# Two of the shared expert's first eight tiles moved from beside the second way back to beside the second path sums

## Chip, cores and metric

The kernel runs on one core of one Trainium2 chip. The metric is the device time of one execution in microseconds (us); several executions are timed and their median is taken. Engines are called as in the profile: PE is TensorE (matmul), PEld its weight loads, DVE is VectorE, ACT is ScalarE, POOL is GpSimd, SP is SyncE, which here issues most DMAs.

## What is computed

Input `x` is (32, 64, 256), the context `ctx` (32, 1601, 256). Three residual blocks follow one another, each on the layer norm of `x`:

```
x = x + xattn(ctx, layernorm(x))     # per sample: euclidean distances, time-warping table, way back,
                                     # context rows of the path summed into the 64 rows they meet
x = x + attn(layernorm(x))           # gated linear recurrence over time, 16 heads, output projection
x = x + ffn(layernorm(x))            # 8 routed experts, top 2 of them, and a shared expert that all rows use
...
def _ffn(x, w1, w2, w3):
    h = jax.nn.silu(x @ w1.T) * (x @ w3.T)
    return h @ w2.T
...
D = _pairwise_euclidean(small, large)
R = _dtw_cost(D)
i_idx, j_idx, valid = _backtrack(R, T_small, T_large)
```

The hidden width of an expert is 704. The 2048 rows of `x` make 16 tiles of 128; the shared expert works on all 16.

## The kernel before

**Alignment.** The 32 samples go in two groups of 16. For a group DVE fills a table step by step (71 steps), and then walks the way back, 71 more steps in which each needs the one before it (L718 shuffle, L719, L724, in the first steps walked also L729). After it a few small operations and one of 1024 columns (L799) write `path_terms`, and a count (`spread`) lets TensorE begin with the group's path sums.

**Path sums** (`add_rows`, TensorE L1469, L1487). They go by pairs of samples, 16 pairs, of which pairs 8 to 15 belong to the second group. A pair has two halves, seven and six 128-row pieces of the context: 14 and 12 matmuls of 256 columns in the program, recorded as 28 and 24 in the trace. Each half needs three things: a mask `on_path`, which TensorE prepares two halves ahead (`path_weigh`, L1465, into banks 2 and 3) and ACT finishes with three activations (`path_mask`, L1200, L1201, L1204); two loads of context rows (`rows_c`), which SP issues into a ring of five (`load_rows`, L1829 and L1832), each when the half that used its slot before has been read (`rows_read`); and a bank that is free. The sums of a pair stand in bank 0 or 1 by turns, and DVE adds them to `xr` (L808).

**Recurrence** (`recurrence(c)`, c from 0 to 3) works on four tiles at once; it uses banks 4 and 5.

**Shared expert** (`experts`, with `up` L1629, `turn` L1640, `down` L1655 on TensorE). A tile is done in two halves of 352 hidden columns. For half h, `up` makes two products into banks 2·(h mod 2) and 2·(h mod 2)+1; ACT takes Silu of the one (L1287, `act_s`), DVE multiplies with the other (L905, `hid`); `turn` transposes the result into bank 6, ACT and DVE copy it out (L1294 and L912, `hidT`); `down` sums into bank 7, and after the second half DVE adds bank 7 to `xr` (L920, `take_output`). The steps run as a pipeline: one step of `experts` is `up` of half h, `turn` of h-1, `down` of h-2, and two more steps drain it.

**Order of the work.** It is written out by hand, the same on each engine. All engines run their programs in order; generators `interleave`, `beside`, `together` and `chain` say after how many steps of one part a step of another comes. The part around the change, which stands alike in the programs of DVE (L1111), ACT (L1377) and TensorE (L1798):

```
interleave(align(1), chain(add_rows(range(0, 4)), together(recurrence(0), add_rows(range(4, 8))),
                           beside(recurrence(1), experts(RUNS[0]), shared_beside), experts(RUNS[1])),
           behind_second)
run(add_rows(range(8, 12)))
run(together(recurrence(2), add_rows(range(12, 16))))
last_recurrence()
```

`RUNS[0]` is tiles 0 to 3 of the shared expert, `RUNS[1]` tiles 4 to 7, `RUNS[2]` tiles 8 to 11, which `last_recurrence` does itself; the routed tiles and tiles 12 to 15 come last. Late in the way back `behind_second` gives one step of `experts` for every four steps of the way back. SP's program has none of the expert's steps and only follows `rows_read` with its loads.

Of the kernel before, what the change touches and what calls it, by code (L numbers as in the profile page):

```python
# [122 lines left out]
def run(steps):  # L123
    for _ in steps:
        pass
# [85 lines left out]


def half_chunks(n):

    return range(n % 2 * CTH, min(CT, (n % 2 + 1) * CTH))
# [11 lines left out]
def rec_order(others):  # L227
# [3 lines left out]

RUNS = [[("shared", t) for t in range(0, 4)], [("shared", t) for t in range(4, 8)],
        [("shared", t) for t in range(8, 12)], [("routed", t) for t in range(MOE_TILES)], [("shared", t) for t in range(12, 16)]]
# [6 lines left out]
def build(nc, x, ctx_nat, ctx_tr, wr_t, wk, wv_t, ww_t, wo_t, gate_t, w1_t, w3_t, w2_t, out):  # L240
    stack = ExitStack()
    with stack:
# [225 lines left out]
        def code_rows(g, q, h):  # L468
            steps = half_steps(q, h)
            return code[g][:, steps[0]:steps[-1] + 1, 0:L]  # L470

        def shared_x(t, k):
# [89 lines left out]
        def vector_program(e):  # L562
# [238 lines left out]
            def add_rows(pairs):  # L801
                for pair in pairs:
                    for _ in range(4):
                        yield
                    e.wait_ge(rows_read, 2 * (pair + 1))
                    if pair == 0:
                        e.wait_ge(x_in, 16)
                    e.tensor_tensor(xr[:, pair, :], xr[:, pair, :], psum[pair % 2][:, 0:D], ALU.add).then_inc(added, 1)  # L808
                    yield
# [89 lines left out]
            def gate_hidden(h):  # L899
                i = h % 2  # L900
                e.wait_ge(upped, 2 * h + 2)
                e.wait_ge(silued, h + 1)
                if h >= 2:
                    e.wait_ge(hid_crossed, h - 1)
                e.tensor_tensor(hid[i][:, :], psum[2 * i + 1][:, 0:HH], act_s[i][:, :], ALU.mult).then_inc(hid_done, 1)  # L905

# [190 lines left out]
            def add_shares():  # L1097
                for n, t in enumerate(SHARES):
                    e.wait_ge(back_in[t // CTILES], 16)
                    e.wait_ge(y_done, UNIT_OF["shared", t if t in (12, 13) else 11] + 1)  # L1100
                    for k in range(2):
# [15 lines left out]
            run(experts(RUNS[3]))  # L1117
            interleave(experts(RUNS[4]), add_shares(), lambda n: 0 if n < 2 else 2 if n < 6 else 3)


        def scalar_program(e):
# [160 lines left out]
            def silu_hidden(h):  # L1282
                i = h % 2
                e.wait_ge(upped, 2 * h + 1)
                if h >= 2:
                    e.wait_ge(hid_done, h - 1)
                e.activation(act_s[i][:, :], psum[2 * i][:, 0:HH], ACT.Silu).then_inc(silued, 1)  # L1287

# [24 lines left out]
            def last_recurrence():  # L1313
# [53 lines left out]
                for unit in range(2, 4):  # L1367
                    for h in range(2):
                        silu_hidden(first[unit] + h)
                    for h in range(2):  # L1370
# [8 lines left out]
                       behind_second)  # L1379
            run(add_rows(range(8, 12)))  # L1380
            run(together(recurrence(2), add_rows(range(12, 16))))
            last_recurrence()
            run(experts(RUNS[3]))
            run(experts(RUNS[4]))


        def tensor_program(e):
# [62 lines left out]
            def path_weigh(n):  # L1450
# [18 lines left out]
            def add_rows(pairs):  # L1469
                for pair in pairs:  # L1470
# [3 lines left out]
                    if pair >= 2:  # L1474
                        e.wait_ge(added, pair - 1)
                    if pair == 8:

                        e.wait_ge(hid_done, 2 * 8)
                    for half in range(2):
# [4 lines left out]
                        for t in half_chunks(half):  # L1484
                            k = min(P, N - t * P)
                            for b in range(2):
                                last = e.matmul(psum[pair % 2][b * T:(b + 1) * T, 0:D],  # L1487
                                                on_path[(2 * pair + half) % 3][0:k, t - half * CTH, b * T:(b + 1) * T],
                                                rows_c[loads[b] % ROWS_RING][0:k, t - half * CTH, :],
                                                start=(t == 0), stop=(t == CT - 1))  # L1490
# [21 lines left out]
            def recurrence(c):  # L1512
# [89 lines left out]
            def up(h, kind, t, half, ex):  # L1602
# [16 lines left out]
                for m in range(2):  # L1619
                    if h >= 2 and m == 0:  # L1620
                        e.wait_ge(silued, h - 1)
                    elif h >= 2:
                        e.wait_ge(hid_done, h - 1)
                    for k in range(KC):
                        if kind == "shared":
                            lhsT, rhs = shared_x(t, k), ws_up[:, m, k, half * HH:(half + 1) * HH]
                        else:
                            lhsT, rhs = srcT[t % 2][:, k, :], w_up[:, bass.ds(ex, 1), m, k, half * HH:(half + 1) * HH]
                        last = e.matmul(psum[2 * i + m][:, 0:HH], lhsT, rhs, start=(k == 0), stop=(k == KC - 1))  # L1629
                    last.then_inc(upped, 1)  # L1630
# [161 lines left out]
            for u in range(GUNITS):  # L1792
                distance_products(u)
                if u in LATENTS_AT:
# [5 lines left out]
                       behind_second)  # L1800
            run(add_rows(range(8, 12)))
            run(together(recurrence(2), add_rows(range(12, 16))))
            last_recurrence()
            run(experts(RUNS[3]))
            run(experts(RUNS[4]))


# [189 lines left out]
```

## Time and profile before

| | |
|---|---|
| median of 3 runs | 1258.32 us (1256.58 to 1264.05) |
| the profiled execution | 1258.05 us, of which the span from first to last instruction is 1256.6 us |
| mean granted TensorE clock | 0.921 of full speed |
| busy: PE, DVE, ACT | 1018.7 us (81%), 703.5 us (56%), 485.3 us (39%) |
| DMA, mean over the span | 143 GB/s |

Stages of the span that matter here, in microseconds from its start: up to 711 the second group's table and way back with other work beside it; 711 to 809 the second group's path sums (together with the recurrence of tiles 8 to 11 from 754 on); 809 to 897 the last recurrence and the routing; from 897 the routed experts and the last shared tiles, in which TensorE is busy without a break.

A timeline row gives start, duration, engine, line, operation, output<-inputs, the shapes and the number of instructions merged in it; in square brackets stands how long the engine was idle before, and what ended that.

### The profile page before, as it was taken

To read this page: it belongs to the slowest core of one execution; us is meant where nothing else is said; L and a number is where in the kernel's file an instruction comes from. 1 tells how busy PE (TensorE), PEld (TensorE's weight loads), DVE (VectorE), ACT (ScalarE), POOL (GpSimd) and SP (SyncE) were. 2 spreads that over 40 slices of the span, in tenths; PEclk is the share of its full clock that TensorE was granted. 3 is DMA by queue.
4 is the path that set the end of the run, shared out by engine and by line. 5 is a ranking of instruction groups with operands and counts; after the bars stand their busy time and mean duration, and the time that the engine had idled before them with its cause. 6 is when DMAs were issued, how large, how long until landed. Compare 5 with 4: busy or idle time off the path is not lost. (4 is left out here: it accounts for less than half of the span.)

```text
span 1256.6 us, 15701 instructions
## 1 busy us (share of the span) xinstructions
PE 1018.7 (81%) x4832; PEld 618.0 (49%) x4832; DVE 703.5 (56%) x2431; ACT 485.3 (39%) x854; POOL 83.6 (7%) x113
## 2 busy tenths in 40 slices
PE   5876636988662599987889578887899999999998
PEld 2332212333220255543656355545677777777776
DVE  5756729999899677496569602346322222222226
ACT  4855434676763244423322144242122222222221
POOL 1000000000000000000000000000122222222210
PEclk9978968999986799989889699889899999999999
DMA  9999974777986979530000098394010011110105
GB/s 365 262 238 289 212 148 134 178 182 177 192 219 99 311 241 329 177 122 1 0 17 1 8 344 277 126 366 170 22 34 31 32 31 34 34 34 30 30 31 192
DMA packets 117407, 179.76 MB, mean 143 GB/s; under 512 B 7600, under 2 KB 91024, under 8 KB 117072
## 3 DMA queue, kind: packets, MB, share of 16 engines
q1 hardware_dynamic: 113584, 168.54, 46.8%
q0 software_dynamic: 3744, 10.23, 2.5%
q8 instruction: 42, 0.69, 0.2%
q14 instruction: 37, 0.30, 0.1%
HBM read 154.32 MB, written 24.42 MB: 142 GB/s over the span
## 5 line engine op out<-in xcount | busy, mean ns | idle before, releaser
L1629 PE MATMUL bank<-w_up,srcT 128*128 x624 | 197.4, 459 | 0.6 <-ACT srcT L1279 0.6
L905 DVE TENSOR_TENSOR hid<-bank,act_s 128x352 f32<-128x352 f32 x110 | 57.4, 524 | 213.6 <-PE bank L1629 208.5
L1416 PE MATMUL bank<-sq,ones 128*64 128x402 f32 (+1 forms) x512 | 107.5, 543 | 48.8 <-ACT sq L1146 48.8
L1629 PEld LDWEIGHTS bank<-w_up,srcT 128*128 128x128 f32 x624 | 117.8, 189 | 54.9 <-issue 0.8
L1287 ACT ACTIVATE act_s<-bank 128x352 f32<-128x352 f32 x110 | 50.8, 464 | 224.5 <-PE bank L1629 224.5
L1432 PE MATMUL bank<-table,ident 128*128 128x402 f32 x144 | 67.1, 550 | 74.1 <-DVE stays L673 67.2
L1410 PE MATMUL bank<-ctxT,latT 128*64 128x402 f32 (+1 forms) x512 | 108.3, 547 | 19.2 <-DMA ctxT<-ctx_tr_dram 18.4
L1655 PE MATMUL bank<-w_dn,hidT 128*128 (+1 forms) x468 | 114.0, 380 | 0.4 <-DVE y_sb L926 0.4
L1487 PE MATMUL bank<-rows_c,on_path 128*64 128x256 f32 (+1 forms) x832 | 100.5, 394 | 11.5 <-DMA rows_c<-ctx_nat_dram 10.7
L1146 ACT ACTIVATE sq<-ctxT 128x1608 f32<-128x1608 f32 x64 | 97.5, 1526 | 11.9 <-DMA ctxT<-ctx_tr_dram 11.9
L1179 ACT ACTIVATE code<-bank,unpassed 128x402 bf16<-128x402 f32 x72 | 42.4, 593 | 135.6 <-PE bank L1434 135.6
L1416 PEld LDWEIGHTS bank<-sq,ones 128*64 128x64 f32 x512 | 36.1, 147 | 116.9 <-ACT sq L1146 78.6
L703 DVE TENSOR_TENSOR_SCAN table<-col_min,table 128x201 f32<-128x201 f32 x140 | 88.6, 633 | 2.6
L1655 PEld LDWEIGHTS bank<-w_dn,hidT 128*128 128x128 f32 (+1 forms) x468 | 83.1, 191 | 8.7 <-issue 0.6
L1629 PE MATMUL bank<-ws_up,h2T 128*128 128x352 f32 x256 | 85.8, 485 | 0.0
L1487 PEld LDWEIGHTS bank<-rows_c,on_path 128*64 128x64 f32 (+1 forms) x832 | 62.5, 141 | 46.4 <-issue 22.3
L1294 ACT ACTIVATE hidT<-bank 128x256 f32<-128x256 f32 x110 | 42.3, 384 | 86.4 <-PE bank L1640 86.4
L1410 PEld LDWEIGHTS bank<-ctxT,latT 128*64 128x64 f32 x512 | 37.0, 147 | 77.0 <-issue 55.1
L1432 PEld LDWEIGHTS bank<-table,ident 128*128 128x128 f32 x144 | 25.6, 203 | 100.0 <-issue 92.3
L696 DVE TENSOR_TENSOR col_min<-table 128x201 f32<-128x201 f32 x142 | 50.9, 359 | 40.0 <-DMA table<-spaced 21.9
L1629 PEld LDWEIGHTS bank<-ws_up,h2T 128*128 128x128 f32 x256 | 51.0, 202 | 25.4 <-issue 4.2
L1433 PE MATMUL bank<-col_min,less 128*128 128x402 f32 x144 | 63.3, 523 | 0.0
(255 smaller groups left out, 1448.5 us busy)
## 6 DMA issues: line engine op xcount, KB each, us to landing
rows_c<-ctx_nat_dram SPq DMA_DIRECT2D x32, 896.0 KB
ctxT<-ctx_tr_dram SPq DMA_DIRECT2D x32, 804.0 KB, 10.0
ctxT<-ctx_tr_dram SPq DMA_DIRECT2D x32, 797.0 KB, 10.7
rows_c<-ctx_nat_dram SPq DMA_DIRECT2D x32, 640.0 KB
table<-spaced SPq DMA_DIRECT2D x16, 896.4 KB, 12.2
spaced<-dist SPq DMA_DIRECT2D x128, 101.0 KB, 6.7
w_up<-w_t_dram SPq DMA_DIRECT2D x16, 704.0 KB, 12.2
w_dn<-w_t_dram SPq DMA_DIRECT2D x16, 256.0 KB, 4.8
```

The source lines that it names most:

```text
L696: e.tensor_tensor(low, prev[:, 1:W], prev[:, 0:L], ALU.min).then_inc(step_done, 1)
L703: e.tensor_tensor_scan(cur[:, 1:W], low, cur[:, 1:W], first, ALU.min, ALU.add).then_inc(step_done, 1)
L905: e.tensor_tensor(hid[i][:, :], psum[2 * i + 1][:, 0:HH], act_s[i][:, :], ALU.mult).then_inc(hid_done, 1)
L1146: e.activation(sq[i][:, :, :, 0:nq], ctxT[ctx_slot(n)][:, :, :, q * QC:q * QC + nq], ACT.Square).then_inc(squared, 1)
L1287: e.activation(act_s[i][:, :], psum[2 * i][:, 0:HH], ACT.Silu).then_inc(silued, 1)
L1410: last = e.matmul(ps[b * T:(b + 1) * T, 0:nq], latT[:, k, pair * P + b * T:pair * P + (b + 1) * T], ctxT[ctx_slot(n)][:, b, k, half * QC:h ...
L1416: last = e.matmul(ps[b * T:(b + 1) * T, 0:nq], ones[:, 0:T], sq[i][:, b, k, 0:nq], start=False, stop=(k == KC - 1))
L1432: e.matmul(gap, ident[:, :], table[g][:, k0 + 1:k0 + n + 1, 0:L], start=True, stop=False)
L1433: e.matmul(gap, less[:, :], col_min[i][:, 2 * h:2 * h + n, :], start=False, stop=False)
L1487: last = e.matmul(psum[pair % 2][b * T:(b + 1) * T, 0:D], on_path[(2 * pair + half) % 3][0:k, t - half * CTH, b * T:(b + 1) * T], rows_c[l ...
L1629: last = e.matmul(psum[2 * i + m][:, 0:HH], lhsT, rhs, start=(k == 0), stop=(k == KC - 1))
L1655: last = e.matmul(psum[7][:, 0:D], hidT[i][0:r, c, :], rhs, start=(half == 0 and c == 0), stop=(half == 1 and c == HC3 - 1))
```

## The change

Tiles 6 and 7 of the shared expert leave the run that is interleaved with the way back and become a run of their own, `RUNS[2]`, beside the path sums of pairs 8 to 11. (The later runs get the numbers 3 to 5, and all units keep their order.) The new rule `path_beside` gives one step of `experts` after the path sums' steps 1, 4, 7, ... (counted from 0; a pair has five). Since banks 0 to 3 are in use by the path sums there, these four halves put their eight products into banks 1, 4 and 5 by turns, and the sums of pairs 8 to 11 all stand in bank 0. With that a pair's sums must wait until the pair before has been added (pairs 9 to 12), pair 8 waits for six tiles rather than eight, pair 12 and the recurrence of tiles 8 to 11 wait until the expert's halves 12 to 15 have been read. SP's and POOL's programs are unchanged.

```
+def path_beside(n):
+
+    return 1 if n % 3 == 1 else 0
...
-RUNS = [[("shared", t) for t in range(0, 4)], [("shared", t) for t in range(4, 8)],
+RUNS = [[("shared", t) for t in range(0, 4)], [("shared", t) for t in range(4, 6)], [("shared", t) for t in range(6, 8)],
...
+        beside_sums = 2 * UNIT_OF["shared", 6]
+
+        def up_bank(h, m):
+
+            if beside_sums <= h < beside_sums + 4:
+                return psum[(1, 4, 5)[(2 * (h - beside_sums) + m) % 3]]
+            return psum[2 * (h % 2) + m]
+
+        def sum_bank(pair):
+            return psum[0 if 8 <= pair < 12 else pair % 2]
...
-            run(add_rows(range(8, 12)))
+            run(beside(add_rows(range(8, 12)), experts(RUNS[2]), path_beside))
...
                 if n == 2 * GTILES:

-                    e.wait_ge(hid_done, 2 * 8)
-                    e.wait_ge(hidT_act, 2 * 8)
-                    e.wait_ge(hidT_dve, 2 * 8)
-                    e.wait_ge(y_done, 8)
+                    e.wait_ge(hid_done, 2 * 6)
...
                     if pair >= 2:
-                        e.wait_ge(added, pair - 1)
-                    if pair == 8:
-
-                        e.wait_ge(hid_done, 2 * 8)
+                        e.wait_ge(added, pair if 9 <= pair <= 12 else pair - 1)
+                    if pair == 8 or pair == 12:
+
+                        e.wait_ge(hid_done, 2 * 6 if pair == 8 else 2 * 8)
...
+                    if c == 2 and h == 0:
+
+                        e.wait_ge(silued, 2 * 8)
+                        e.wait_ge(hid_done, 2 * 8)
...
-                    if h >= 2 and m == 0:
+                    job = 2 * (h - beside_sums) + m
+                    if 0 <= job < 3:
+                        if m == 0:
+
+                            e.wait_ge(hid_done, beside_sums)
+                            e.wait_ge(h2_turned, 4)
+                            e.wait_ge(gate_own, GATE_OWN + 1)
+                    elif 3 <= job < 8:
+                        e.wait_ge(silued, h) if m else e.wait_ge(hid_done, h - 1)
+                    elif h >= 2 and m == 0:
                         e.wait_ge(silued, h - 1)
```

How the instructions move is shown at two places. The first is DVE within the second way back, where a step of `experts` stood between two steps of it (L718 to L724 are one step; `hid`, `hidT` and the sum into `xr` are the expert's). Before:

```order
L718 STREAM_SHUFFLE beyond<-threshold_68 128x1
L719 SCALAR_TENSOR_TENSOR beyond<-row_53,threshold_68 128x201
L724 ISA passed,threshold_68<-beyond,code_107 128x202
L724 ISA threshold_68 128x1
L905 TENSOR_TENSOR hid_152<-bank,act_s_150 128x352
L912 COPY hidT_153<-bank 96x128
L920 TENSOR_TENSOR xr<-xr,bank 128x256
L718 STREAM_SHUFFLE beyond<-threshold_68 128x1
```

The same place after the change (its lines are 16 higher):

```order
L734 STREAM_SHUFFLE beyond<-threshold_68 128x1
L735 SCALAR_TENSOR_TENSOR beyond<-row_53,threshold_68 128x201
L740 ISA passed,threshold_68<-beyond,code_107 128x202
L740 ISA threshold_68 128x1
L936 TENSOR_TENSOR xr<-xr,bank 128x256
L734 STREAM_SHUFFLE beyond<-threshold_68 128x1
```

Here tile 5 is being drained: its last sum stays, while the multiplication and the copy of tile 6 are gone. Over the whole way back four `hid`, four `hidT` and two `xr` go.

The second place is TensorE between the sums of pair 9 and those of pair 10 (the number after `bank` is the bank's own). Before:

```order
L1487 MATMUL bank1<-rows_c3_142,on_path1_145 64x256
L1487 MATMUL bank1<-rows_c4_143,on_path1_145 64x256
L1465 MATMUL bank2<-path_terms_147,row_terms_148 128x128 x4
L1465 MATMUL bank3<-path_terms_147,row_terms_148 128x128 x2
L1487 MATMUL bank0<-rows_c0_139,on_path2_146 64x256
L1487 MATMUL bank0<-rows_c1_140,on_path2_146 64x256
```

After:

```order
L1478 MATMUL bank3<-path_terms_147,row_terms_148 128x128 x2
L1655 MATMUL bank4<-ws_up_169,h2T1_172 128x352 x2
L1655 MATMUL bank5<-ws_up_169,h2T1_172 128x352 x2
L1666 MATMUL bank6<-ident_49,hid1_152 128x128 x2
L1666 MATMUL bank6<-ident_49,hid1_152 96x128
L1681 MATMUL bank7<-ws_dn_170,hidT0_153 128x256 x3
L1655 MATMUL bank1<-ws_up_169,h2T1_172 128x352 x2
L1655 MATMUL bank4<-ws_up_169,h2T1_172 128x352 x2
L1666 MATMUL bank6<-ident_49,hid0_151 128x128 x2
L1666 MATMUL bank6<-ident_49,hid0_151 96x128
L1681 MATMUL bank7<-ws_dn_170,hidT1_154 128x256 x3
L1500 MATMUL bank0<-rows_c0_139,on_path2_146 64x256
```

Two whole steps of `experts` (the third and the fourth of the six) now stand in this one place. The others stand singly: an `up` after the first half of pair 8, `up` and `turn` after its second half, `turn` and `down` after pair 10, a last `down` after the first half of pair 11.

## Rows read from the trace of the kernel before

**Rows 1.** The page: its first line.

```profile
span 1256.6 us, 15701 instructions
```

**Rows 2.** Windows: stretch, us, busy of PE, PEld, DVE, ACT, POOL, clock, DMA share, GB/s.

```profile
656.00:695.00 39.00, 34.76 (x131) 23.52 (x132) 36.61 (x200) 6.43 (x16) 0.00 (x0) 0.94 0.00 1
711.00:720.00 9.00, 7.05 (x42) 4.45 (x42) 0.39 (x1) 3.73 (x6) 0.00 (x0) 0.55 0.01 2
730.00:740.00 10.00, 6.99 (x52) 4.83 (x48) 0.42 (x1) 2.67 (x4) 0.00 (x0) 0.83 1.00 348
750.00:760.00 10.00, 7.60 (x75) 5.46 (x72) 2.68 (x10) 5.01 (x8) 0.00 (x0) 1.00 1.07 370
772.00:790.00 18.00, 17.65 (x69) 7.88 (x69) 3.83 (x8) 8.79 (x14) 0.00 (x0) 1.00 0.50 168
```

**Rows 3.** Timeline of DVE in the second way back, eight of its steps.

```profile
671.52 0.52 DVE L905 TENSOR_TENSOR hid<-bank,act_s 128x352 f32<-128x352 f32 x1
671.96 0.28 DVE L912 COPY hidT<-bank 96x128 f32<-96x128 f32 x1
672.17 0.15 DVE L718 STREAM_SHUFFLE beyond<-threshold 128x1 f32<-128x1 f32 x1
...
673.11 0.15 DVE L718 STREAM_SHUFFLE beyond<-threshold 128x1 f32<-128x1 f32 x1
...
675.80 0.52 DVE L905 TENSOR_TENSOR hid<-bank,act_s 128x352 f32<-128x352 f32 x1
...
680.41 0.52 DVE L905 TENSOR_TENSOR hid<-bank,act_s 128x352 f32<-128x352 f32 x1
```

**Rows 4.** Timeline of PE, one step of `experts` where nothing stands between.

```profile
908.32 2.53 PE L1629 MATMUL bank<-w_up,srcT 128*128 x8
910.69 0.49 PE L1640 MATMUL bank<-ident,hid 128*128 128x128 f32 x3
911.02 1.46 PE L1655 MATMUL bank<-w_dn,hidT 128*128 x6
912.32 2.53 PE L1629 MATMUL bank<-w_up,srcT 128*128 x8
```

**Rows 5.** Timeline of PE over the path sums of pairs 8 to 13.

```profile
711.45 0.93 PE L1465 MATMUL bank<-path_terms,row_terms 128*128 128x128 f16 x7 [9.96 <-DVE path_terms L799]
...
714.67 5.39 PE L1487 MATMUL bank<-rows_c,on_path 128*64 128x256 f32 x28 [0.34 <-issue]
719.99 0.56 PE L1465 MATMUL bank<-path_terms,row_terms 128*128 128x128 f16 x7
720.49 2.81 PE L1487 MATMUL bank<-rows_c,on_path 128*64 128x256 f32 x24
723.24 0.51 PE L1465 MATMUL bank<-path_terms,row_terms 128*128 128x128 f16 x6
725.03 3.24 PE L1487 MATMUL bank<-rows_c,on_path 128*64 128x256 f32 x28 [1.29 <-DMA rows_c<-ctx_nat_dram]
728.21 0.56 PE L1465 MATMUL bank<-path_terms,row_terms 128*128 128x128 f16 x7
729.05 2.81 PE L1487 MATMUL bank<-rows_c,on_path 128*64 128x256 f32 x24 [0.28 <-DMA rows_c<-ctx_nat_dram]
...
735.31 4.93 PE L1487 MATMUL bank<-rows_c,on_path 128*64 128x256 f32 x28 [3.01 <-DMA rows_c<-ctx_nat_dram]
...
763.74 3.24 PE L1487 MATMUL bank<-rows_c,on_path 128*64 128x256 f32 x28 [1.62 <-DMA rows_c<-ctx_nat_dram]
```

**Rows 6.** The tile of context rows, 700 to 816: what its matmuls waited for.

```profile
  DMA rows_c<-ctx_nat_dram: 10.7, 9
```

**Rows 7.** DMA issues 711 to 809 (KB each), and a piece of the chain (start, us).

```profile
rows_c<-ctx_nat_dram SPq DMA_DIRECT2D x13, 896.0 KB
rows_c<-ctx_nat_dram SPq DMA_DIRECT2D x14, 640.0 KB
...
rows_c<-ctx_nat_dram SPq DMA_DIRECT2D x14, 65.0 KB
...
720.09 4.80 DMA rows_c<-ctx_nat_dram
```

**Rows 8.** Timeline of ACT and DVE: a copy, one mask's three activations, one sum.

```profile
694.98 0.38 ACT L1294 ACTIVATE hidT<-bank 128x256 f32<-128x256 f32 x1 [3.89 <-PE bank L1640]
...
743.96 0.60 ACT L1200 ACTIVATE on_path<-bank 128x512 f32<-128x512 f32 x1 [1.13 <-PE bank L1465]
744.45 0.38 ACT L1201 ACTIVATE on_path<-bank 128x256 f32<-128x256 f32 x1
744.87 0.93 ACT L1204 ACTIVATE on_path<-on_path,ones 128x768 f32<-128x768 f32 x1
752.32 0.42 DVE L808 TENSOR_TENSOR xr<-xr,bank 128x256 f32<-128x256 f32 x1 [8.37 <-PE bank L1487]
```

More of the change, by code:

```diff
@@ L807, in add_rows @@
                         e.wait_ge(x_in, 16)
-                    e.tensor_tensor(xr[:, pair, :], xr[:, pair, :], psum[pair % 2][:, 0:D], ALU.add).then_inc(added, 1)
+                    e.tensor_tensor(xr[:, pair, :], xr[:, pair, :], sum_bank(pair)[:, 0:D], ALU.add).then_inc(added, 1)
                     yield
@@ L904, in gate_hidden @@
                     e.wait_ge(hid_crossed, h - 1)
-                e.tensor_tensor(hid[i][:, :], psum[2 * i + 1][:, 0:HH], act_s[i][:, :], ALU.mult).then_inc(hid_done, 1)
+                e.tensor_tensor(hid[i][:, :], up_bank(h, 1)[:, 0:HH], act_s[i][:, :], ALU.mult).then_inc(hid_done, 1)
             def turn_hidden(h):
@@ L1113, in vector_program @@
                        behind_second)
-            run(add_rows(range(8, 12)))
+            run(beside(add_rows(range(8, 12)), experts(RUNS[2]), path_beside))
             run(together(recurrence(2), add_rows(range(12, 16))))
             last_recurrence()
-            run(experts(RUNS[3]))
-            interleave(experts(RUNS[4]), add_shares(), lambda n: 0 if n < 2 else 2 if n < 6 else 3)
+            run(experts(RUNS[4]))
+            interleave(experts(RUNS[5]), add_shares(), lambda n: 0 if n < 2 else 2 if n < 6 else 3)
         def scalar_program(e):
@@ L1286, in silu_hidden @@
                     e.wait_ge(hid_done, h - 1)
-                e.activation(act_s[i][:, :], psum[2 * i][:, 0:HH], ACT.Silu).then_inc(silued, 1)
+                e.activation(act_s[i][:, :], up_bank(h, 0)[:, 0:HH], ACT.Silu).then_inc(silued, 1)
             def turn_hidden(h):
@@ L1379, in scalar_program @@
                        behind_second)
-            run(add_rows(range(8, 12)))
+            run(beside(add_rows(range(8, 12)), experts(RUNS[2]), path_beside))
             run(together(recurrence(2), add_rows(range(12, 16))))
             last_recurrence()
-            run(experts(RUNS[3]))
             run(experts(RUNS[4]))
+            run(experts(RUNS[5]))
         def tensor_program(e):
@@ L1486, in add_rows @@
                             for b in range(2):
-                                last = e.matmul(psum[pair % 2][b * T:(b + 1) * T, 0:D],
+                                last = e.matmul(sum_bank(pair)[b * T:(b + 1) * T, 0:D],
                                                 on_path[(2 * pair + half) % 3][0:k, t - half * CTH, b * T:(b + 1) * T],
@@ L1628, in up @@
                             lhsT, rhs = srcT[t % 2][:, k, :], w_up[:, bass.ds(ex, 1), m, k, half * HH:(half + 1) * HH]
-                        last = e.matmul(psum[2 * i + m][:, 0:HH], lhsT, rhs, start=(k == 0), stop=(k == KC - 1))
+                        last = e.matmul(up_bank(h, m)[:, 0:HH], lhsT, rhs, start=(k == 0), stop=(k == KC - 1))
                     last.then_inc(upped, 1)
@@ L1800, in tensor_program @@
                        behind_second)
-            run(add_rows(range(8, 12)))
+            run(beside(add_rows(range(8, 12)), experts(RUNS[2]), path_beside))
             run(together(recurrence(2), add_rows(range(12, 16))))
             last_recurrence()
-            run(experts(RUNS[3]))
             run(experts(RUNS[4]))
+            run(experts(RUNS[5]))
         def sync_program(e):
```

## The prediction, as written before the run

> **What bounds the kernel now.** I read the page first, for the span of 1256.6 us [rows 1]; then the chain of waits, to see in which stage which engine ends last; then the windows, stage by stage; then the timelines of DVE, TensorE and ACT in the two stages that the change touches. The order of the two programs says what moved, never how long it takes.
>
> Two stages matter. In the second way back DVE sets the pace. In the 39.0 us from 656 to 695 DVE is busy for 36.61, and TensorE, at 34.76, works in the gaps that DVE's order gives it [rows 2]. No wait of DVE's stands between the steps: a step without an insert takes 673.11 - 672.17 = 0.94 us, and the timeline shows the next one starting at once [rows 3]. TensorE ends its share early and is idle for 9.96 us before the path sums can begin at 711.45 [rows 5]. So what DVE sheds here comes off the time, and what TensorE sheds does not.
>
> In the path sums that follow, the loads of context rows set the pace. TensorE waits for them nine times, 10.7 us in total [rows 6], and they move 370 GB/s at a full DMA share [rows 2]. From about 768 on the recurrence of tiles 8 to 11 joins in, and TensorE is the bound: 17.65 us busy of 18.0 [rows 2]. After that nothing of the change is left; whatever TensorE is late with at 768 it stays late with to the end.
>
> **Term 1: what the way back sheds.** A tile puts two steps of the expert between eight steps of the way back. From 671.52 to 680.41 is one such tile, 8.89 us; eight bare steps are 8 x 0.94 = 7.52; so a tile costs the way back 1.37 us, less than the durations of its five instructions together, because part of them fills the small gap between two dependent steps [rows 3]. Two tiles leave: 2 x 1.37 = 2.74 us. I bound it by 1.8 (if two of the inserts had filled gaps that stay) and 3.4 (four `hid`, four `hidT`, two sums into `xr` at their start-to-start distances of 0.44, 0.21 and 0.33). ACT's and TensorE's shares there were under cover and bring nothing. The path sums should start at 711.93 rather than 714.67.
>
> **Term 2: what TensorE has to do more afterwards.** One step of the expert at full clock goes from 908.32 to 912.32: 2.37 for the `up`, 0.33 for the `turn`, 1.30 for the `down`, 4.00 us in all [rows 4]. Four halves are 16.0 us. They enter a stretch where TensorE had been waiting. What it can swallow is in the rows.
>
> **Term 3: how much of it the waits take.** I walk TensorE's order. A pair at full clock, taken from start to start, is 3.18 for the first half, 0.50 for the next weighing, 2.75 for the second half, 0.45 for its weighing: 6.88 us [rows 5].
>
> From pair 8 to the start of pair 10, before: 735.31 - 714.67 = 20.64 us, in which 1.29 + 0.28 + 3.01 = 4.58 us are waits for loads [rows 5]. After: the same without these waits is 16.06; the first four steps of the expert (4 `up`, 3 `turn`, 2 `down`) add 9.48 + 0.99 + 2.60 = 13.07. That is 29.1 us. The five loads that are in the ring at the start and the four that follow have 29 us for what took under 21, so no load is late. Pair 10 starts at 711.93 + 29.1 = 741.1, that is 5.75 later than before.
>
> From pair 10 to the start of pair 13, before: 763.74 - 735.31 = 28.43 us [rows 5]. After, two roads lead there. TensorE's: three pairs, 20.64; the last two steps of the expert, 2.93; and two waits. The first is new: the `hidT` of half 15 stands on ACT behind a mask of 1.84 us (744.87 + 0.93 - 743.96), then 0.38 for it [rows 8], then DVE's copy and the sum of pair 10, 0.28 and 0.42 [rows 3, 8], and pair 11 now waits for that sum, because all four pairs use bank 0. With the hand-overs that is 2.9 us from the end of the weighing, of which 1.63 is covered by TensorE's own `turn` and `down`: 1.3 us seen. The second, at pair 12, is the sum of pair 11 alone, 0.42 and its hand-over less a weighing of 0.45: 0.4 seen. The road is 25.3 us. The loads' road: at pair 10 the ring is full, so nine loads must still pass before pair 13, five of 896 KB and four of 640 + 65 KB [rows 7], 7.47 MB; at 370 GB/s that is 20.2 us, after the first half of pair 10 (3.2) and a latency of 2.3 (the 4.80 us from issue to landing less the 2.48 that 896 KB take at that rate [rows 7]). 25.7 us. Neither road is met alone: a late load delays the next issue, which is why pairs before took some 9.5 us where the bytes ask for 8.8. I take the middle between the longer road and the 28.43 of before, 27.0, less a trace for the clock dip below: 26.9.
>
> Pair 13 then starts at 741.1 + 26.9 = 768.0 against 763.74 [rows 5]: 4.2 us later. The ends are 25.7 and 28.43, that is 3.0 and 5.75 later. (In other words: of 16.0 us some 9 vanish in waits and 2.7 come back from the way back.)
>
> **The clock.** The granted clock was 0.83 in 730 to 740, after the wait of 3.01 us, and the first half of pair 10 took 4.93 us instead of 3.24; in 711 to 720 it was 0.55 and the first half of pair 8 took 5.39 [rows 2, 5]. So each time TensorE fell to 1.2 GHz for a while. The 1.7 us at pair 10 are in the 28.43 above and should go, since TensorE no longer stands before pair 10; that is part of why I end below that figure. The 2.15 us at pair 8 I keep, though TensorE will now have been idle for some 28 us rather than 10 before it (the drained steps end near 680). The Trainium skill, page "TensorE: Matmul & The Clock Gate", section "HAM oscillation — how this bites in real kernels", says that waits for loads let the clock fall and that keeping the array busy across them holds it up; at pair 10 the trace agrees with its 0.83, and by that rule the dip goes as I have it, while without it the sum would be 1.7 us more.
>
> **The other edits.** The three banks by turns: each of the eight products needs a bank whose reader finished a whole step earlier; the nearest are the two adjoining steps, which follow each other as in the routed stage, where a step takes 4.00 us without a wait [rows 4]. I take 0, and bound it by 0 and 1. The waits at pair 12 and at the recurrence find everything read long ago: 0. ACT gets four Silu and four copies, some 3.4 us, into a stretch where it is busy for 5.01 of 10 [rows 2]: hidden, but for the mask above. No load is issued earlier or later for another reason than `rows_read`.
>
> **The sum.** -2.74 + 16.0 - 9.1 = +4.2 us on the profiled execution's 1258.05, that is 1262.25; the median of the runs is 0.27 above that execution, so 1262.5.
>
> **Rivals.**
> A. *The waits swallow all they can.* All 10.7 us of waits for loads, the 1.7 of the dip and the 2.15 of the cold start vanish: 16.0 - 14.55 - 2.74 = -1.3 us, 1257. For it speaks that the ring is full when the expert's steps end; against it that the loads after pair 10 have the same 7.47 MB to move and that the steps stand in the first half of the stretch.
> B. *The cold start lasts longer.* TensorE idles nearly three times as long before pair 8. If it stays at 1.2 GHz through the first two `up` and the second half of pair 8, then 2.37 + 2.75 + 2.37 us run at half speed and cost up to 7.5 more: 1270. For it: 0.55 in 711 to 720 [rows 2]. Against: 9.96 us of idle already led to the lower level, and it cannot go below that. Half of that price, 1266, is the likelier form.
> C. *The turns do not turn (slower by over 1%).* At each of five places TensorE waits for ACT's mask, then Silu or copy, then DVE: about 3 us that I take as covered everywhere but once. If the cover of an `up` were missing in all of them, 5 x 3 = 15 us come on top: 1277. It would decide from 1.7 us of idle time per step (8.4 us in all) on. Against it: the masks are made two halves ahead, and ACT has half its time free [rows 2].
>
> **Chances.** Forecast 0.62, A 0.16, B 0.13, C 0.06, something else 0.03. A measurement of this kernel tells about 1%, 12.6 us, from no change. The forecast, A and nearly all of B lie within it; C and the end of B give slower 0.06; nothing here reaches 12 us faster, which leaves 0.02 for what I don't see. The range takes in A with a microsecond of scatter, and B's likelier form with three: 1256 to 1269.
>
> **What would show it.** The path sums of pair 8 should start near 711.9, and pair 10 near 741, with no wait for a load before it and a clock of 1.00 there. Waits of the `rows_c` matmuls for DMA should fall from 10.7 us to about 3, all after pair 10. TensorE should wait for DVE's sum before pair 11, by 1 to 1.5 us. From pair 13 to the end everything should lie 4 us later and else be unchanged. I am wrong if the start of pair 8 has moved by less than 1.8 or more than 3.4, if waits for ACT or DVE add up to more than 4 us between pairs 8 and 12, or if the stage after pair 13 changes its own length.

## The result

| | median | runs |
|---|---|---|
| before | 1260.93 us (1250.46 to 1271.03) | 18 |
| changed | 1268.24 us (1258.36 to 1276.47) | 18 |

The ratio is 1.0059, with a 95% interval of 1.0030 to 1.0088: 7.4 us slower (3.8 to 11.1), within the 1% that the prediction calls no change. The two profiled executions differ by more: the span of the changed kernel's is 14.6 us over the 1256.6 of [rows 1]. How much of that is the change and how much the single execution is the question of what follows.

The page of the changed kernel begins, against [rows 1]:

```profile
span 1271.2 us, 15702 instructions
```

The windows of the changed kernel, against [rows 2] (stretch, us, busy of PE, PEld, DVE, ACT, POOL, clock, DMA share, GB/s):

```profile
695.00:711.00 16.00, 0.22 (x3) 0.23 (x4) 14.47 (x78) 0.00 (x0) 0.00 (x0) 0.50 0.00 0
711.00:720.00 9.00, 7.50 (x50) 4.89 (x49) 0.00 (x0) 4.17 (x7) 0.00 (x0) 0.63 0.00 0
730.00:740.00 10.00, 10.00 (x69) 6.75 (x66) 1.14 (x3) 4.57 (x8) 0.00 (x0) 1.00 0.91 303
740.00:750.00 10.00, 10.00 (x82) 6.62 (x82) 1.23 (x3) 3.19 (x6) 0.00 (x0) 1.00 0.42 142
```

TensorE now does nothing in the last 16 us of the way back (its 0.22 us lie behind 710.78), and works without a break from 730 to 750, at full clock, where before it was busy for 6.99 of the first 10 us at 0.83 and for 8.19 of the second 10 at 1.00. The loads moved 348 and 299 GB/s in these two windows before, and 303 and 142 now: they wait for TensorE to read what they brought.

TensorE's timeline over the pairs' first halves and the places where steps of the expert came in, against [rows 5]:

```profile
710.78 0.93 PE L1478 MATMUL bank<-path_terms,row_terms 128*128 128x128 f16 x7 [25.01 <-DVE path_terms L815]
...
714.00 5.03 PE L1500 MATMUL bank<-rows_c,on_path 128*64 128x256 f32 x28 [0.34 <-issue]
...
719.37 2.59 PE L1655 MATMUL bank<-ws_up,h2T 128*128 128x352 f32 x8
...
727.82 3.24 PE L1500 MATMUL bank<-rows_c,on_path 128*64 128x256 f32 x28
...
734.58 2.59 PE L1655 MATMUL bank<-ws_up,h2T 128*128 128x352 f32 x8
737.00 0.49 PE L1666 MATMUL bank<-ident,hid 128*128 128x128 f32 x3
737.33 1.46 PE L1681 MATMUL bank<-ws_dn,hidT 128*128 128x256 f32 x6
738.63 2.53 PE L1655 MATMUL bank<-ws_up,h2T 128*128 128x352 f32 x8
...
742.72 3.24 PE L1500 MATMUL bank<-rows_c,on_path 128*64 128x256 f32 x28
...
752.49 3.24 PE L1500 MATMUL bank<-rows_c,on_path 128*64 128x256 f32 x28 [1.21 <-DVE xr L824]
...
765.88 2.81 PE L1500 MATMUL bank<-rows_c,on_path 128*64 128x256 f32 x24 [1.15 <-DMA rows_c<-ctx_nat_dram]
...
770.38 3.24 PE L1500 MATMUL bank<-rows_c,on_path 128*64 128x256 f32 x28 [1.25 <-DMA rows_c<-ctx_nat_dram]
```

Pair 8 starts at 714.00, pair 10 at 742.72, pair 13 at 770.38. Two steps of the expert take 742.72 - 734.58 = 8.1 us including a short hand-over, against the 4.00 us each of [rows 4], so the turns of banks 1, 4 and 5 cost nothing. Pair 11 waits for DVE for 1.21 us. What the row names as DVE is a chain of three engines, here from the end of ACT's mask to TensorE:

```profile
750.58 0.94 ACT L1220 ACTIVATE on_path<-on_path,ones 128x768 f32<-128x768 f32 x1
751.42 0.36 ACT L1310 ACTIVATE hidT<-bank 128x256 f32<-128x256 f32 x1
751.82 0.29 DVE L928 COPY hidT<-bank 96x128 f32<-96x128 f32 x1 [8.58 <-ACT hidT L1310]
752.03 0.41 DVE L824 TENSOR_TENSOR xr<-xr,bank 128x256 f32<-128x256 f32 x1
```

The matmuls' waits for loads, 10.7 us in [rows 6], have shrunk to this (the tile of context rows, what it waited for):

```profile
  DVE xr L824: 3.2, 3
  DMA rows_c<-ctx_nat_dram: 2.6, 3
```

The first of these rows counts matmuls and weight loads together. Of the matmuls alone only one waited for DVE, pair 11's, 1.2 us.

**Where the 14.6 us are.** I cut every profile at the same events, so that stages can be compared whatever came before them: A, up to the `down` of the shared expert before which TensorE waits 4.41 us for DVE (655.77 before, the row below); B, from there to the end of `path_terms`; C, from the start of pair 8 (always 3.28 us later) to the crossing of the recurrence's rows (`ident,hn`) right behind the first half of pair 13; D, from there to the first routed `up`; E, the rest. The 3.28 us between B and C are in no column but in the span.

```profile
655.77 2.90 PE L1655 MATMUL bank<-ws_dn,hidT 128*128 128x256 f32 x6 [4.41 <-DVE hidT L912]
```

| profile | A | B | C | D | E | span |
|---|---|---|---|---|---|---|
| before | 655.8 | 55.6 | 52.6 | 131.4 | 357.9 | 1256.6 |
| changed | 657.8 | 52.9 | 60.0 | 139.4 | 357.9 | 1271.2 |
| difference | +2.0 | -2.7 | +7.3 | +8.0 | 0.0 | +14.6 |

A holds no change at all, so its difference is scatter. B and C hold the change. D has the same instructions in the same order, and was a surprise.

### The profile page after: what moved, and what is told of

It is laid out like the page before. It is cut to its first block, busy times and chain, and to the rows that moved or that the text cites. A ratio compares the mean times of both kernels' runs of the same rounds, so it can differ in the third digit from the quotient of the medians.

```text
span 1271.2 us, 15702 instructions
## 1 busy us (share of the span) xinstructions
PE 1027.0 (81%) x4832; PEld 624.0 (49%) x4832; DVE 705.2 (55%) x2431; ACT 484.3 (38%) x854; POOL 83.6 (7%) x113
## 4 chain that ended last, share of the span: by engine, by line
PE 40%; DVE 7%; ACT 1%; issue 1%; DMA 1%; DVEq 0%; ACTq 0%
PE bank L1655 18%; PE bank L1681 10%; PE bank L1500 3%; PE bank L1666 3%; PE bank L1521 2%; DVE beyond L735 2%; DVE passed L740 1%; DMA rows_c<-ctx_nat_dram 1%; PE bank L1615 1%; DVE beyond L734 1%; PE bank L1771 1%; PE bank L1478 1%; PE bank L1583 0%; PE bank L1601 0%; DVE hid L921 0%
## 5 line engine op out<-in xcount | busy, mean ns | idle before, releaser
L1500 PEld LDWEIGHTS bank<-rows_c,on_path 128*64 128x64 f32 (+1 forms) x832 | 59.2, 139 | 41.7 <-issue 13.6
```

Source lines behind the costliest of these rows:

```text
L1500: last = e.matmul(sum_bank(pair)[b * T:(b + 1) * T, 0:D], on_path[(2 * pair + half) % 3][0:k, t - half * CTH, b * T:(b + 1) * T], rows_c[l ...
```

## The experiments

Two profiles of one kernel are needed before a difference between two kernels means anything, so the first two runs repeat both.

**The kernel before, again.** No edit.

> The kernel before once more, unchanged. In the two profiles at hand the stretch from the end of pair 15 to the first routed tile took 90.1 us before and 96.7 us in the changed kernel, with the same instructions in the same order and a granted clock of 0.91 and 0.80 (817 to 913 us). Theory (that part is chance: where the clock falls differs from execution to execution): here the same stretch differs from 90.1 by 2 us or more, or the clock in it does. Rival (the change causes it): 90.1 within 0.5 us again.

A 653.0, B 55.6, C 51.8, D 134.2, span 1255.7 us. The stretch that the expectation speaks of took 91.6 us, 1.5 more than in the first profile, which is less than the 2 us that the theory asked for and more than the 0.5 that the rival allowed; D, which also takes in pairs 13 to 15, is 2.7 us longer. So D does scatter. B agrees to 0.1 us, and C to 0.9. The slow first half that pair 10 had in [rows 5] (4.93 us) is found at pair 11 here (4.62), so the place of this dip is not fixed either.

**The changed kernel, again.** No edit.

> The changed kernel once more, unchanged. Theory (chance): the stretch from the end of pair 15 to the first routed tile lies away from 96.7 us by 2 us or more, anywhere between 90 and 97; the stretch from pair 8 to pair 13 is again 56.4 within 0.5 us, since there TensorE does not stand still long enough for its clock to fall. Rival (the change causes the longer end stretch): 96.7 within 1 us again.

A 655.1, B 52.9, C 60.7, D 137.3, span 1267.2 us. B is -2.7 again, C is +9.0 against the second profile of before, and D is 2.1 us away from the first. From pair 8 to pair 13 it took 57.2 us, outside the 56.4 within 0.5 that was expected. The end stretch took 94.6 us, 2.1 less than the first time, just over the 2 us that the theory of chance had asked for. Yet D is longer in both profiles of the changed kernel than in both of before, which makes chance alone a weak explanation; the later runs take that up. Nearly all of the difference lies behind pair 15: that stretch took 90.1 and 91.6 us before, 96.7 and 94.6 in the changed kernel.

**Half of the change.** Only tile 7 moves.

```
-[("shared", t) for t in range(4, 6)], [("shared", t) for t in range(6, 8)],
+[("shared", t) for t in range(4, 7)], [("shared", t) for t in range(7, 8)],
...
-        beside_sums = 2 * UNIT_OF["shared", 6]
+        beside_sums = 2 * UNIT_OF["shared", 7]
...
-                    e.wait_ge(hid_done, 2 * 6)
+                    e.wait_ge(hid_done, 2 * 7)
```

> The change by half: only tile 7 of the shared expert moves beside the path sums, tile 6 stays beside the way back. Theory (what counts is how much TensorE work the waits for loads can swallow, some 9 us of it): the way back gains 1.37 us instead of 2.7; of 8.0 us of TensorE work added nearly all is swallowed, the stretch from pair 8 to pair 13 takes 50 to 51 us (before 49.1, changed 56.4), and the sum against the kernel before is -0.7 to +0.5 us. Rival (the steps cost by their number, through hand-overs and the bank turns, not by TensorE's time): half the loss of the changed kernel, so 52.7 us for the stretch and about +2.3 us in all.

B 54.2, C 54.6, D 131.1; ratio 1.0007 (0.9977 to 1.0037). B falls by 1.4 us, half of 2.7. C grows by 2.4 against the mean of before's two profiles (52.2), where two tiles make it grow by 8.1 (60.3). From the start of pair 8 to that of pair 13 it is 51.0 us, as the theory had it, against the rival's 52.7. The first tile costs 2.4 us and the second 5.8, so it isn't the number of steps that costs but what TensorE can still hide. The waits for loads fall only to 5.8 us, as its row on the context tile says:

```profile
  DMA rows_c<-ctx_nat_dram: 5.8, 5
```

B and C together are +1.0 us, a little over the -0.7 to +0.5 that I expected, and the timing cannot tell it from zero.

**The fifth step one place later.**

```
-    return 1 if n % 3 == 1 else 0
+    return 1 if n in (1, 4, 7, 10, 14, 16) else 0
```

> The changed kernel with one step of the expert one place later: path_beside gives the fifth step after the path sums' step 14 rather than 13, so that DVE adds pair 10 before it copies hidT of half 15. Theory (a pair in the one bank waits on DVE's order, behind an ACT mask): the wait of 1.21 us before pair 11 goes, and from the start of pair 8 to the start of pair 13 it takes 55.2 us instead of 56.4. Rival (that wait only hides a wait for loads that comes anyway): the DVE wait goes, waits for loads grow from 2.6 to about 3.8 us, and the stretch stays at 56.4.

DVE now adds pair 10 first, and the wait of 1.21 us before pair 11 is gone. The waits for loads are longer instead. The rows show pairs 11, 12 and 13:

```profile
751.77 3.24 PE L1500 MATMUL bank<-rows_c,on_path 128*64 128x256 f32 x28
...
760.63 3.24 PE L1500 MATMUL bank<-rows_c,on_path 128*64 128x256 f32 x28 [0.58 <-DMA rows_c<-ctx_nat_dram]
...
766.40 2.81 PE L1500 MATMUL bank<-rows_c,on_path 128*64 128x256 f32 x24 [2.04 <-DMA rows_c<-ctx_nat_dram]
...
771.19 3.24 PE L1500 MATMUL bank<-rows_c,on_path 128*64 128x256 f32 x28 [1.53 <-DMA rows_c<-ctx_nat_dram]
```

The waits add up to 4.15 us against 2.63 in the first profile of the changed kernel. From pair 8 to pair 13 it took 56.8 us, not 55.2, and C is 60.3 us, the mean of the changed kernel. The rival holds: the new wait on DVE was real and cost nothing, because from pair 11 on the loads are the bound again. The ratio, 1.0032 (0.9994 to 1.0069), overlaps that of the changed kernel.

**Only the banks.** The kernel before with all sums of pairs 8 to 11 in bank 0.

```
+        def sum_bank(pair):
+            return psum[0 if 8 <= pair < 12 else pair % 2]
...
-                        e.wait_ge(added, pair - 1)
+                        e.wait_ge(added, pair if 9 <= pair <= 12 else pair - 1)
```

> The kernel before, with only the banks of the change: the sums of pairs 8 to 11 all in bank 0, and pairs 9 to 12 waiting for the sum of the pair before. Theory (DVE's addition of 0.42 us lies under the next weighing and the wait for loads): from pair 8 to pair 13 49.1 us as before, within 0.4. Rival (the one bank is a good part of the loss): four hand-overs of 0.4 us or more, 50.7 us or over.

C 52.1 us, between the two profiles of before, with 10.0 us of waits for loads. From pair 8 to pair 13 it took 48.5 us, a little less than the 49.1 within 0.4 that was expected, and far from the rival's 50.7. One bank for four pairs is free in the kernel before; in the changed kernel it led to the wait before pair 11.

**The steps spread over the four pairs.**

```
-    return 1 if n % 3 == 1 else 0
+    return 1 if n in (1, 4, 9, 11, 14, 19) else 0
```

> The changed kernel with its six steps of the expert spread over the four pairs (after the path sums' steps 1, 4, 9, 11, 14, 19 rather than 1, 4, 7, 10, 13, 16). Theory (16 us of TensorE work against some 10 us of waits: the rest stays on the path wherever it stands; only the 1.2 us before pair 11 and part of the last 2.6 us of waits for loads can be had): 54.5 to 55.5 us from pair 8 to pair 13 instead of 56.4. Rival (the loss comes from two steps back to back before pair 10, which empty the loads' ring of work): 52 us or less.

Neither came: from pair 8 to pair 13 it took 58.4 us, and C is 62.0, longer than the 60.0 and 60.7 of the changed kernel, and the ratio 1.0099 (1.0066 to 1.0132), an interval that overlaps that of the changed kernel. What I had not priced is seen in its timeline up to pair 12 and, in a piece of the chain (start, us), in the load behind it:

```profile
757.90 0.56 PE L1478 MATMUL bank<-path_terms,row_terms 128*128 128x128 f16 x7
758.39 2.81 PE L1500 MATMUL bank<-rows_c,on_path 128*64 128x256 f32 x24
761.14 0.51 PE L1478 MATMUL bank<-path_terms,row_terms 128*128 128x128 f16 x6
761.48 1.52 PE L1681 MATMUL bank<-ws_dn,hidT 128*128 128x256 f32 x6
765.47 4.93 PE L1500 MATMUL bank<-rows_c,on_path 128*64 128x256 f32 x28 [2.47 <-DMA rows_c<-ctx_nat_dram]
```

```profile
758.01 7.33 DMA rows_c<-ctx_nat_dram
```

Pair 12's second load was asked for when the first half of pair 11 had been read, at 758.0, and landed at 765.3: over 7 us, in which TensorE had 5 us of work. From 745 to 755, while steps of the expert ran, the DMA share was 0.61 (186 GB/s). I read this as a ring too short for TensorE to use a lead: the loads stood still while the steps of the expert ran, and were late when they had ended. A longer ring was not tried, so this is argued from the rows and not shown. The wait also made the clock fall (4.93 us rather than 3.24), and these 1.7 us are the whole difference between this C and the changed kernel's. Such a fall isn't a mark of this order alone: a later profile, of the changed kernel with a delay that comes only behind the first half of pair 13, has one too, at that half, after a wait of 2.14 us. What is shown is that spreading the steps gains nothing.

**Additional matmuls before the path sums,** in both kernels, so that TensorE comes warm to pair 8, that is at 2.4 GHz.

```
                 if n == 2 * GTILES:
+                    e.wait_ge(h2_turned, 4)
+                    e.wait_ge(gate_own, GATE_OWN + 1)
+                    e.wait_ge(back_done, GROUPS * BACK_INCS - 3 * 8)
+                    for _ in range(14):
+                        e.matmul(psum[4][:, 0:HH], ident[:, :], ws_up[:, 0, 0, 0:HH], start=True, stop=True)
```

> The kernel before, and on TensorE, eight steps of the way back before its end, 14 additional matmuls of 128x352 into bank 4 whose result nobody reads (the output is the same). Question: what the cold start of the path sums costs. Theory (TensorE comes to pair 8 at 1.2 GHz only because it was idle for 10 us; warmed, it runs at 2.4): the first half of pair 8 takes 3.2 us instead of 5.4, and from the end of the way back to the start of pair 9 some 2.5 us go, but nearly all of it turns up again as waits for loads until pair 13, since the loads set the pace there: 0 to 1 us in all. Rival (the start sets when the loads begin, so that all of it is kept): 2.5 us less at pair 13 and at the end. Other rival (the additional matmuls are themselves late): pair 8 starts later than DVE's path_terms by over 1.5 us, and it is slower.

> The changed kernel with the same 14 additional matmuls before the path sums (the output is the same). Theory (here TensorE is the bound from pair 8 to pair 13, not the loads): the 2 us that the cold half of pair 8 costs are kept whole, the stretch from pair 8 to pair 13 takes 54.4 us instead of 56.4 if the loads are not met earlier, at least 55. Rival (after 25 us of idle 14 matmuls don't bring the clock back): the first half of pair 8 stays near 5 us.

Here I made a mistake: the lines stand behind `path_weigh`'s own wait for `spread`, so the matmuls ran after `path_terms` and not beside the way back. Both kernels start pair 8 some 10 us late, and are slower: ratios 1.0102 (1.0059 to 1.0145) and 1.0145 (1.0078 to 1.0211). That is the other rival of the first text, by my own hand. The stage behind it can still be read. Kernel before with the additional matmuls:

```profile
715.11 10.79 PE L1461 MATMUL bank<-ws_up,ident 128*128 128x352 f32 x28 [9.96 <-DVE path_terms L799]
...
728.59 3.24 PE L1492 MATMUL bank<-rows_c,on_path 128*64 128x256 f32 x28 [0.64 <-issue]
...
745.98 4.93 PE L1492 MATMUL bank<-rows_c,on_path 128*64 128x256 f32 x28 [1.87 <-ACT on_path L1204]
```

The first half of pair 8 is down to 3.24 us, so in this kernel the cold start came from the idle time before it, and it costs 2.2 us of TensorE's time. (The row of pair 10 names ACT, but its mask had been ready for 3 us; the wait is for a load.) But C is 52.8 us against 52.6 and 51.8: nothing is kept, since the loads set the pace, and the clock falls later instead, at pairs 10, 11 and 12.

In the changed kernel the same matmuls did not bring a warm start:

```profile
726.09 0.49 PE L1483 MATMUL bank<-path_terms,row_terms 128*128 128x128 f16 x6 [1.16 <-ACT on_path L1217]
727.23 4.93 PE L1505 MATMUL bank<-rows_c,on_path 128*64 128x256 f32 x28 [0.65 <-issue]
...
775.52 4.93 PE L1505 MATMUL bank<-rows_c,on_path 128*64 128x256 f32 x28 [1.63 <-DMA rows_c<-ctx_nat_dram]
...
785.82 4.93 PE L1505 MATMUL bank<-rows_c,on_path 128*64 128x256 f32 x28 [1.69 <-DMA rows_c<-ctx_nat_dram]
```

The granted clock was back at 1.00 from 719 to 727, but fell again as pair 8 began, after waits of 1.16 and 0.65 us. The kernel before went through the same two waits (1.16 and 0.64 us) at full clock. So the rival's number came, a first half of about 5 us, though not for the rival's reason, and this run does not say what a warm start would be worth in the changed kernel. Its C is 63.9 us, 3.5 more than the mean of the changed kernel's two profiles, and the two further falls of the clock, at pairs 12 and 13 with 1.7 us each, account for that.

**Delays before stage D.** The same matmuls, 13 and 7 in the kernel before, 4 and 7 in the changed one, at the crossing behind pair 13.

```
                 for h in range(2):
...
+                    if c == 2 and h == 0:
+                        for _ in range(13):
+                            e.matmul(psum[4][:, 0:HH], ident[:, :], ws_up[:, 0, 0, 0:HH], start=True, stop=True)
```

> The kernel before, with 13 additional matmuls of 128x352 into bank 4 before the recurrence of tiles 8 to 11 crosses its rows (0.59 us each at full clock, 7.7 us in all; nobody reads them, the output is the same). Question: the profiles of kernels without the change took 130 to 135 us from that crossing to the first routed tile, those with it 136 to 139, with the same instructions. Theory (the change delays this stage against the moment at which the clock rose at pair 8 by some 8 us, and the distance from there decides which of its waits are followed by a fall of the clock): less the 7.7 us the stage takes 136 us or more here too, and the w_r and w_w matmuls about 120 us behind pair 8, at full clock in all kernels without the change, are slow. Rival (something in the changed kernel itself): less the 7.7 us 130 to 135 us, and those matmuls stay fast.

> The same with 7 additional matmuls, 4.1 us. Theory (distance from pair 8): the pattern of slow matmuls differs from that of the kernel before as well as from that with 7.7 us, and the stage less 4.1 us may be shorter or longer than 130 to 135. Rival: 130 to 135 less the 4.1 us, with the known pattern.

> The changed kernel with 4 additional matmuls at the same place, 2.4 us. Theory (distance from pair 8): the slow w_r and w_w matmuls about 120 us behind pair 8, or the slow w_o ones at 141, become fast or others become slow; less the 2.4 us the stage need not be 136 to 139 us. Rival: 136 to 139 with the known pattern.

> The changed kernel with 7 additional matmuls, 4.1 us. Theory (distance from pair 8): another pattern again, the stage less 4.1 us away from 136 to 139. Rival: 136 to 139 with the known pattern.

All profiles, in us. From C the additional matmuls are taken off at their full-clock time (2.4, 4.1, 7.7); those in front of pair 8 lie outside C:

| | C | D |
|---|---|---|
| before, twice | 52.6, 51.8 | 131.4, 134.2 |
| before, one bank | 52.1 | 135.2 |
| before, 14 matmuls ahead of pair 8 | 52.8 | 130.2 |
| half of the change | 54.6 | 131.1 |
| before, delays of 4.1 and 7.7 | 54.7, 52.6 | 134.0, 134.0 |
| changed, twice | 60.0, 60.7 | 139.4, 137.3 |
| changed, fifth step later | 60.3 | 136.6 |
| changed, spread | 62.0 | 135.5 |
| changed, 14 matmuls ahead of pair 8 | 63.9 | 139.4 |
| changed, delays of 2.4 and 4.1 | 60.7, 62.6 | 132.7, 136.1 |

C scatters too. Up to pair 13 the rows "twice" and "delays" are profiles of the same instructions, four of each kernel: 51.8 to 54.7 before, 60.0 to 62.6 changed. The longest of each has a first half at the low clock that the others lack or have shorter (6.11 us at pair 12, 4.93 us at pair 13). The means differ by 8.1 us.

A delay of 2.4 us goes with a stage D of 132.7 us in the changed kernel, 4.6 and 6.7 less than without it. That is a whole kernel that does more and takes less from pair 8 to the first routed tile: 195.8 us, with the delay, against 199.3 and 198.0. This is one profile, and of the four delays the only one with a D that its kernel doesn't also show without a delay: 134.0 us, twice in the kernel before, is within the 130 to 135 of the rivals, and 136.1 in the changed kernel within the 136 to 139. The difference is in which matmuls are slow. TensorE in the changed kernel's second profile:

```profile
821.79 6.37 PE L1655 MATMUL bank<-ws_up,h2T 128*128 128x352 f32 x16
...
830.34 1.09 PE L1745 MATMUL bank<-ident,hn 128*128 128x128 f32 x8 [2.18 <-DVE hn L627]
...
833.53 3.62 PE L1521 MATMUL bank<-hT,w_r 128*128 128x512 f32 x4
836.94 2.54 PE L1521 MATMUL bank<-hT,w_w 128*128 128x512 f32 x4
...
852.71 6.67 PE L1771 MATMUL bank<-w_o,kv 128*128 128x256 f32 x16 [2.93 <-DVE kv L989]
```

The same place in the second profile of before, and then in the changed kernel with the delay of 2.4 us:

```profile
813.62 7.50 PE L1629 MATMUL bank<-ws_up,h2T 128*128 128x352 f32 x16
...
822.17 1.10 PE L1719 MATMUL bank<-ident,hn 128*128 128x128 f32 x8 [1.05 <-DVE hn L611]
...
825.05 1.88 PE L1508 MATMUL bank<-hT,w_r 128*128 128x512 f32 x4
826.77 1.88 PE L1508 MATMUL bank<-hT,w_w 128*128 128x512 f32 x4
```

```profile
827.12 7.57 PE L1658 MATMUL bank<-ws_up,h2T 128*128 128x352 f32 x16
...
835.66 1.09 PE L1748 MATMUL bank<-ident,hn 128*128 128x128 f32 x8 [0.98 <-DVE hn L627]
...
838.54 1.88 PE L1521 MATMUL bank<-hT,w_r 128*128 128x512 f32 x4
```

The projections take 1.88 us at 2.4 GHz and up to 3.62 at 1.2. The two profiles of each kernel agree in these rows, and all five profiles with both tiles moved and no delay have the slow `w_r`, which speaks against a pattern drawn afresh in each execution. The rows ahead of it go with it in all 14 profiles: where the two `up` took 7.4 to 8.0 us, because the clock rose late in them (in the second profile of before it is 0.50 up to 818.0, 4.4 us after their start), the wait for DVE that follows is 0.6 to 1.2 us and `w_r` is fast; where they took 6.3 to 6.8 us (in the changed kernel's second it is 0.85 from 824.0 to 826.0, 2.2 us after their start), that wait is 1.7 to 2.2 us and `w_r` is slow. TensorE gets nothing for an early rise of the clock, since DVE's `hn` comes at nearly the same time in all (15.6 to 16.2 us behind the end of pair 15), and the clock falls behind the longer wait. What decides when the clock rises in the `up` is not shown.

The prediction for 7.7 us in the kernel before failed by its number: 136 us or more was expected and 134.0 came, which is the rival's number, with the `w_r` matmuls at 3.0 us slower than in before but `w_w` fast. So the distance from pair 8 is not all of it. That the time of stage D goes with which matmuls run at the low clock is shown; that a mere delay moves it rests on one profile; what rule sets it stays open.

## Why the prediction was right, and where not

- **Term 1, the way back.** Predicted -2.74 us, between -1.8 and -3.4; measured -2.7 in both pairs of profiles, and -1.4 for one tile. The reading of start-to-start distances, rather than durations, was right. (The upper bound of 3.4 is mis-summed, its own terms give 3.3; nothing hangs on it.)
- **Term 2, 16.0 us of TensorE work.** The steps took what they take in the routed stage; banks and turns cost nothing, as taken.
- **Term 3, what the waits take.** From pair 8 to pair 10 the walk gave 29.1 us, and 28.7 and 28.9 were measured; from pair 10 to pair 13 it gave 26.9, and 27.7 and 28.2 were measured. The wait before pair 11 was put at 1.3 us and measured at 1.21, and it turned out to cost nothing, because the loads would have come no sooner. That the 26.9 came near is in part luck: it was the middle between a road of 25.7 and the 28.43 of before, not worked out, and the measured times lie toward the upper end. Of the 16.0 us, 9.1 were to vanish in waits; C grew by 7.3 and 9.0, so 8.7 and 7.0 did. Taken at the same events, B and C together are +4.6 us in the first pair of profiles and +6.2 in the second, against the 4.2 predicted. A part of what the second pair has more is that the kernel before has the shorter C there (51.8 against the 52.6 of the profile I read).
- **The clock.** The dip before pair 10 went, as said, and neither profile of the changed kernel has another one up to pair 13. The cold half of pair 8 was 5.03 and 5.25 us after 25 to 26 us of idle, no longer than the 5.39 after 10, and the `up` behind it took 2.59 us, so rival B is refuted.
- **The step that failed:** "After that nothing of the change is left; whatever TensorE is late with at 768 it stays late with to the end." Stage D came out 8.0 and 3.1 us longer. The list of what would prove me wrong named it (the stage after pair 13 changes its own length), and I had charged nothing for a later start as such. How much it adds to the measured 7.4 us is not settled: B and C are +5.4 us on the mean of the two pairs of profiles, which leaves 2.0 for D, while in the profiles D differs by 5.5. What the runs show in place of the step is a stage whose length depends on where in it TensorE's clock is low; they don't show why the change moves that.
- Rival A is refuted: 2.6 to 3.1 us of waits for loads stayed. Rival C is refuted: no step of the expert waited for ACT or DVE, and of the path sums only pair 11, as named.
- **The time itself.** 1268.24 us lies in the range of 1256 to 1269 by 0.8 us, and the room up there had been made for rival B, which did not come. Of the 5.7 us between 1262.5 and 1268.24, 2.6 are the kernel before, whose median was 1260.93 here and not 1258.32, and 3.1 are the change.

No version tried beats the kernel before. Half of the change can't be told from it; of the versions with both tiles moved that were timed more than once, all are slower or, for the fifth step later, not told from it.

## What to carry to other kernels

Idle time of an engine is worth filling only up to what it adds up to where the work is put. Here 16 us went into a stretch that, with its clock dip, had 12 to give and gave 8, and came out of one where the moved work cost the bound engine 2.7: work that is under cover of a slower engine lies well where it is. Spreading the moved work over the waits did not hide more of it, and a buffer ring that is refilled only as it is read is the likely reason. And with executions of one kernel that lie up to 20 us apart, two kernels are told apart by cutting their profiles at common events: B agreed to 0.1 us where the spans of one kernel differed by 4.

## What the runs showed of the hardware

The granted clock fell after waits as short as 1.6 us in one place (the first half of pair 12 in the changed kernel with matmuls ahead of pair 8, 4.93 us) and stayed up after 2.55 us in another (the `ones,val` matmuls of tiles 8 to 11 in the kernel before with these matmuls, 1.92 us). The length of the wait alone does not decide it: those `ones,val` matmuls wait 2.54 or 2.55 us in every profile and took 1.92 us in the first of before and 3.54 in the second. The second of before has its slow half at pair 11 and the first at pair 10, and the `w_o` matmuls of the last recurrence took 3.69, 5.38 and 6.67 us behind the same wait of 2.93 us.

In the last recurrence, on the other hand, two executions of one kernel show nearly the same slow matmuls, and with a delay of 2.4 us in front of the stage they were others: 132.7 us for unchanged instructions that took 139.4 and 137.3 without it. Over all kernels tried the stage took from 130 to 139 us. I had not expected a change to be paid for, or paid back, 60 us behind the place where it was made.
